# Transposing DMAs issued by ScalarE, reloads in pieces, and one scatter-add per shared slot in a routed decoder layer

## The chip, the cores and the metric

The kernel runs on one core of a Trainium2 chip. The metric is the device time of one execution in microseconds (us), taken as the median of several runs.

## The reference

A decoder layer on x of 8 x 256 tokens of width 256: a gated projection of the normalized rows, a retention over a context, and a feed-forward part in which every token is sent to two of eight experts.

```python
x = x + gate_block(layernorm(x))                     # WB, WBf, gamma = sigmoid(...)
x = x + retention(layernorm(x), ctx, ctx)            # Wq, Wk, Wv, xpos, decay mask
# feed-forward, on u = layernorm(x), added to x with its own skip
xn = rms_norm(u, norm_scale)
scores = einsum('bsd,ed->bse', xn, w_router)
_, ids = top_k(scores, 2); c = softmax(scores) at ids
h = einsum('bsd,ehd->bseh', xn, w_up)                # 8 experts, 2 x 704 columns
val, gate = split(h, 2); h = val * silu(gate)
y = einsum('bseh,edh->bsed', h, w_down)
out = sum over the two experts of a token of y * c, + u
```

## The kernel before

The kernel has three parts. Parts A and B (`step_a`, `step_b`, one step for a batch of 256 tokens) do the gated projection and the retention; B also stores the normalized rows, as fp16 high and low parts, and the softmax values in `xrow_hbm`, and the skip in `out`. The routing chain then sorts the 4096 pairs of token and expert: a chain of small VectorE instructions (`link`, each waits for the one before it), 32 columns of pairs (25 by VectorE, 7 by ScalarE) multiplied on TensorE into the slot table (L1404), from which come `take_idx` (rows to gather) and `add_idx` (rows to add to). A second chain and a product give `slot_expert` and `slot_home`, the expert of each slot and where its weights lie; `s_te` tells that they are ready. TensorE runs filler products (`keep_clock`, L1245) between the groups of this stage.

The expert part has 36 slots of 128 rows in the order `ORDER`. 32 slots belong to one expert. Four are mixed: 64 rows of one expert, 64 of another, with the weights of the second expert copied next to them (`half_up`, `half_dn`). The mixed ones stand at positions 28, 30, 32 and 34. In step r the engines do for slot i = r-1 (`step_e`):

- GpSimd gathers the rows of a slot by an indirect DMA (`take`, L808) into `xs`, two buffers, and adds the result of a slot to `out` by an indirect DMA with addition (L824). Its queue holds in order: wait for `yt` of slot j, wait until the add of slot j-1 has landed, add of j, take of j+4. A take waits for the transposes of the slot two before it.
- SyncE waits for the rows and transposes them by DMA (L485) into `xsT`, two buffers, when the up products of slot i-2 are done. The same queue reloads, step by step, the weights of the experts in the order of their rank (`fetch_up`, 1.4 MB, `fetch_down`), and copies the half weights.
- TensorE: first up product of slot i (L1437), transposes of h of slot i-1 (L1484), the other two up products of slot i, down product of slot i-1 (L1453).
- ScalarE, in this order: y of slot i-2 out of its bank, scaled, into `yt` (L682); silu of the first gate columns (L694); a part of the transposed h (L699); the high part of a reloaded weight (`up_high` L633, `down_high` L639, for r up to 22); silu of the tail (L711); the fp16 high parts of h (L714, L716); in each third step the second half of `down_high`.
- VectorE: the other part of the transposed h (L1183), h = value times silu (L1194), the low parts of h (L1198 to L1201), the scale of the pairs (L1161), the low part of the weights (L917, L923).

A token may have both its experts in the two halves of one mixed slot. An addition DMA that names one row twice would lose one of the two, so a mixed slot is added by two DMAs, one for each half, with the rows of the other half sent to unused rows behind `out` (`half_idx[:, m]`).

## Time and profile before

| | before |
|---|---|
| median of 3 runs | 418.7 us (412.5 to 421.2) |
| the profiled execution | 418.5 us |
| its span | 416.7 us |
| TensorE busy (matmul) | 356.8 us, 86% |
| VectorE, ScalarE, GpSimd busy | 262.8, 235.8, 177.3 us |
| granted clock of TensorE, mean | 0.958 |

The profiler records one execution. The span is the time from its first to its last instruction. The granted clock is the share of its full speed at which TensorE may run. A row of the busy table by stretch has: from and to in us, the length, busy us and count of TensorE's matmuls, of its weight loads, of VectorE, of ScalarE and of GpSimd, then the granted clock, the mean busy share of the 16 DMA engines and the GB/s that they moved. In the other views PE is TensorE, DVE VectorE, ACT ScalarE, POOL GpSimd, SP SyncE; a q behind the name is the engine's queue (register loads, DMA issues). L682 is line 682 of the kernel. An entry in square brackets is the idle time of the engine before the instruction, and what ended it.

### The profile page before, as it was taken

How to read it: one execution, taken by the hardware profiler on the slowest of the kernel's cores; microseconds unless marked ns; L12 is line 12 of the kernel's file. 1: busy time of each engine (PE TensorE's matmuls, PEld its weight loads, DVE VectorE, ACT ScalarE, POOL GpSimd, SP SyncE). 2: the span in 40 equal slices, each digit the busy share in tenths (PEclk: the TensorE clock that was granted, in tenths of full speed). 3: DMA queues.
4: the chain of work that ended last, by engine and by line, in shares of the span. 5: the costliest groups of instructions: out<-in, count | busy, mean ns of one | idle time of the engine just before them, and what ended most of it. 6: DMA issues, size and time to landing. Idle time of an engine off the chain costs nothing.

```text
span 416.7 us, 9007 instructions
## 1 busy us (share of the span) xinstructions
PE 356.8 (86%) x2494; PEld 256.8 (62%) x2494; DVE 262.8 (63%) x714; ACT 235.8 (57%) x432; POOL 177.3 (43%) x183
## 2 busy tenths in 40 slices
PE   5699989999998068797997999899999999988930
PEld 5588878888885053464655566566665666655620
DVE  2799755665567886686676667687775654544410
ACT  3377686677764663575765567577654544433410
POOL 2545544455557302165253434545434334445341
PEclk9899999999999559999999999999999999999995
DMA  7999823444433103968969896444368954776421
GB/s 233 409 424 407 320 101 104 150 153 152 151 102 102 53 5 94 247 178 227 255 170 219 248 226 184 79 78 65 65 177 186 259 71 107 224 207 138 48 28 24
DMA packets 48107, 69.48 MB, mean 167 GB/s; under 512 B 24608, under 2 KB 40864, under 8 KB 46144
## 3 DMA queue, kind: packets, MB, share of 16 engines
q1 hardware_dynamic: 39984, 58.17, 43.1%
q0 software_dynamic: 7536, 10.24, 16.6%
q10 hardware_dynamic: 544, 0.52, 0.4%
q8 instruction: 23, 0.38, 0.4%
q14 instruction: 20, 0.16, 0.1%
HBM read 45.79 MB, written 9.63 MB: 133 GB/s over the span
## 4 chain that ended last, share of the span: by engine, by line
PE 47%; DMA 28%; issue 8%; DVE 7%; POOL 4%; ACT 2%; SPq 1%; DVEq 1%; POOLq 1%; ACTq 0%
PE bank L1437 13%; DMA out<-arena,add_idx 9%; PE bank L1453 6%; DMA out<-arena,half_idx 6%; DMA arena<-xrow_hbm,take_idx 5%; DMA arena<-arena 4%; PE bank L1291 3%; PE bank L1252 3%; PE bank L1254 3%; PE bank L1345 3%; PE bank L1354 3%; PE bank L1484 2%; PE bank L1236 2%; POOL out L824 2%; DMA expert_w<-in_wup 2%
## 5 line engine op out<-in xcount | busy, mean ns | idle before, releaser
L1437 PE MATMUL bank<-expert_w,arena 128*128 x576 | 124.6, 362 | 10.2 <-DMA arena<-arena 9.0
L824 POOL DMA_INDIRECT out<-arena,add_idx x32 | 55.2, 1725 | 107.7 <-ACT arena L682 48.9
L1437 PEld LDWEIGHTS bank<-expert_w,arena 128*128 128x128 f16 x576 | 54.0, 98 | 60.1 <-issue 14.0
L1453 PE MATMUL bank<-expert_w,arena 128*128 x544 | 64.8, 273 | 1.7 <-DVE arena L1183 1.4
L1194 DVE SCALAR_TENSOR_TENSOR arena<-bank,scales,arena 128x512 f32<-128x512 f32 x72 | 41.6, 583 | 34.8 <-ACT arena L711 19.9
L1453 PEld LDWEIGHTS bank<-expert_w,arena 128*128 128x128 f16 x544 | 52.2, 98 | 13.5 <-issue 4.9
L808 POOL DMA_INDIRECT arena<-xrow_hbm,take_idx x36 | 37.8, 1050 | 30.5 <-DVE add_idx L1141 12.6
L694 ACT ACTIVATE arena<-bank,scales 128x512 f32<-128x512 f32 x36 | 24.7, 686 | 43.5 <-PE bank L1437 36.9
L1183 DVE COPY arena<-bank 128x1024 f16<-128x1024 f16 x36 | 24.7, 687 | 18.9 <-PE bank L1484 18.7
L711 ACT ACTIVATE arena<-bank,scales 128x192 f32<-128x192 f32 x36 | 15.1, 420 | 34.0 <-PE bank L1437 25.9
L917 DVE SCALAR_TENSOR_TENSOR expert_w<-expert_w,scales 128x1408 f16<-128x1408 f32 (+2 forms) x18 | 27.1, 1520 | 9.5 <-issue 9.2
L1484 PEld LDWEIGHTS bank<-ident,arena 128*128 128x128 f16 x396 | 24.6, 98 | 12.2 <-ACT arena L716 3.2
L770 POOL TENSOR_TENSOR arena<-arena 128x512 f32<-128x512 f32 x16 | 20.4, 1272 | 23.3 <-DVE arena L1019 18.7
L1484 PE MATMUL bank<-ident,arena 128*128 128x128 f16 x396 | 28.0, 219 | 2.5 <-ACT arena L716 1.7
L633 ACT ACTIVATE expert_w<-expert_w,scales 128x1408 f16<-128x1408 f32 (+1 forms) x16 | 23.4, 1467 | 9.7 <-issue 6.4
L1198 DVE TENSOR_TENSOR arena<-arena 128x512 f16<-128x512 f32 x36 | 24.9, 692 | 4.8 <-ACT arena L714 1.7
L682 ACT ACTIVATE arena<-bank,arena 128x256 f32<-128x256 f32 x36 | 16.9, 469 | 18.1 <-PE bank L1453 15.1
L511 ACT ACTIVATE squares<-expert_w,front 128x1408 bf16<-128x1408 f32 x16 | 23.4, 1460 | 0.0
L714 ACT ACTIVATE arena<-arena 128x512 f16<-128x512 f32 x36 | 22.4, 622 | 1.1 <-DVE arena L1194 1.0
L824 POOL DMA_INDIRECT out<-arena,half_idx x8 | 12.6, 1570 | 21.8 <-DMA out<-arena,half_idx 11.9
L983 DVE TENSOR_TENSOR arena<-bank,cst_b 128x512 f32<-128x512 f32 x16 | 11.0, 690 | 15.3 <-PE bank L1345 11.5
L1252 PE MATMUL bank<-front,arena 128*128 128x258 f32 x64 | 17.5, 398 | 1.0 <-ACT arena L542 1.0
(228 smaller groups left out, 668.0 us busy)
## 6 DMA issues: line engine op xcount, KB each, us to landing
expert_w<-in_wup SPq DMA_DIRECT2D x15, 1408.0 KB, 10.0
expert_w<-in_wdn SPq DMA_DIRECT2D x15, 640.0 KB, 4.4
expert_w<-expert_w SPq DMA_DIRECT2D x4, 704.0 KB, 5.1
expert_w<-in_x SPq DMA_DIRECT2D x8, 256.0 KB, 7.7
arena<-in_ctxT SPq DMA_DIRECT2D x8, 256.0 KB, 3.0
out<-expert_w SPq DMA_DIRECT2D x8, 256.0 KB, 2.5
expert_w<-in_wdn SPq DMA_DIRECT2D x30, 64.0 KB, 4.3
expert_w<-expert_w SPq DMA_DIRECT2D x2, 768.0 KB, 3.6
```

The lines of the kernel that those rows point to most:

```text
L511: nc.scalar.activation(squares[:, 0:2 * H], raw_up(n // 2 + 1, n % 2), ACT.Square, scale=ns_s[:, n % 2:n % 2 + 1], accum_out=sums[:, n:n + ...
L694: nc.scalar.activation(sg[:, 0:HA], bank[0][:, 0:HA], ACT.Silu, scale=gate_scale).then_inc(s_sg, 1)
L808: pool.indirect_dma_start(out=xs_row[:, i % 2], out_offset=None, in_=xrow_hbm, in_offset=bass.IndirectOffsetOnAxis(ap=take_idx[:, ORDER[i] ...
L824: pool.indirect_dma_start(out=out, in_=yt[:, i % 2], in_offset=None, out_offset=bass.IndirectOffsetOnAxis(ap=rows_of, axis=0), compute_op= ...
L917: V.scalar_tensor_tensor(out=up_part(k, c, 1)[:, lo:lo + n], in0=up_source(k, c, e)[:, lo:lo + n], scalar=up_scale[:, ds(e * 2 + c, 1)], i ...
L1183: V.tensor_copy(hT[:, 0:8], hT_bank[0]).then_inc(s_hTa, 1)
L1194: V.scalar_tensor_tensor(out=hh[:, cols], in0=src, scalar=value_scale, in1=sg[:, cols], op0=ALU.mult, op1=ALU.mult).then_inc(s_h, 1)
L1198: V.tensor_tensor(hs_low, hh[:, 0:HA], hs_high[:, 0:HA], ALU.subtract).then_inc(s_hlo, 1)
L1252: T.matmul(dst, uT[:, 2 * slot + c, j * P:(j + 1) * P], wb_s[:, c], start=c == 0, stop=False)
L1437: last = T.matmul(bank[q][:, 0:n], x, split_w[:, ds(home + (c * UPC + at_w), n)], **flags)
L1453: last = T.matmul(y, h, split_w[:, ds(home + dn_at(c, w), D)], **flags)
L1484: last = T.transpose(hT_bank[c // 8][:, c % 8], hs[:, c * P:(c + 1) * P], ident16[:, :])
```

## The change

- `transpose_rows`: the transposing DMAs of slots 1 to 35 leave SyncE's queue and go to ScalarE's. That of slot 1 stands ahead of the first step, that of slot i+2 in the step of slot i, between the tail silu and the fp16 copies, behind a wait for the gathered rows.
- SyncE: one piece per turn. `fetch_up(k, c)` loads one half of the up weights (0.7 MB), so that ranks 1 to 7 are spread over turns 1 to 21 instead of 1 to 14; each half has its own semaphore. The up halves of mixed slots are copied one per turn too.
- Mixed slots: their scaled y goes to `y_mixed`, is multiplied on TensorE by `same_row` (1 where two entries of the slot name the same row of `out`), and is copied from the bank into `yt`. Rows of the upper half that are there twice are sent to an unused row. One addition DMA does the slot. `added(n)` becomes 16 n.
- Routing: the number of the first expert is computed behind the columns, and ScalarE's `up_high` for it, too; the chain of ranks stands behind `add_idx`; the entry constants are computed in step 1 of part B, from a scan in place of a constant; weight scales and routing constants swap their steps; one filler product less.

```diff
         def added(n):
-            return 16 * (n + sum(mixed(i) for i in range(n)))
+            return 16 * n
 
         def dn_at(c, low):
             return 2 * UPC + (c // 3) * DNC + low * DNH + (c % 3) * D
 
-        MARK_LINKS, COL_LINKS, TILE_LINKS, TABLE_LINKS = 13, 34, 35, 48
+        MARK_LINKS, COL_LINKS, TILE_LINKS, TABLE_LINKS = 13, 32, 33, 48
         DVE_COLS = 2 * NT - 7
...
-        HALF_UP_AFTER, HALF_DOWN_AFTER = (23, 25, 30, 32), (24, 26, 31, 33)
+        HALF_UP_AFTER, HALF_DOWN_AFTER = (23, 26, 30, 33), (25, 28, 32, 35)
...
-            def fetch_up(k):
+            def fetch_up(k, c):
                 sp.wait_ge(s_te, 1)
                 sp.wait_ge(s_lo, 4)
                 e = table_entry(slot_expert, UNIFORM + 2 * MIXED + k, NE - 1)
-                sp.dma_start(expert_w[:, (k + 1) * EXP:(k + 1) * EXP + UPC], wup[ds(e, 1)].squeeze(0)).then_inc(s_fup[k], 16)
+                sp.dma_start(raw_up(k + 1, c), wup[ds(e, 1)].squeeze(0)[:, c * 2 * H:(c + 1) * 2 * H]).then_inc(s_fup[k % 2][c], 16)
...
-            def copy_half_up(q):
+                    sp.dma_start(dst[lo:lo + HLAST, tail:DNC], src[0:HLAST, tail:DNC]).then_inc(s_fdn[k % 2], 16)
+
+            def copy_half_up(q, c):
                 if q < 2:
                     sp.wait_ge(s_lo, 2 * NE + 2)
                 else:
                     sp.wait_ge(s_up, 3 * ORDER.index(UNIFORM + q - 2) + 3)
                 home = table_entry(slot_home, UNIFORM + MIXED + q, (NE - 1) * 2 * EXP)
-                for c in range(2):
-                    sp.dma_start(half_up[q % 2][c], split_w[:, ds(home + c * UPC, UPC)]).then_inc(s_hup[q], 16)
+                sp.dma_start(half_up[q % 2][c], split_w[:, ds(home + c * UPC, UPC)]).then_inc(s_hup[q], 16)
 
             def copy_half_down(q):
                 if q < 2:
@@ -479,19 +483,18 @@
                 sp.dma_start(half_dn[q % 2], split_w[:, ds(home + 2 * UPC, 2 * DNC)]).then_inc(s_hdn[q], 16)
 
             for i in range(1, NSLOT):
-                sp.wait_ge(s_xs[i % 2], 16 * (i // 2) + 16)
                 if i >= 2:
                     sp.wait_ge(s_up, 3 * i - 3)
-                sp.dma_start_transpose(xsT[:, i % 2], xs[:, i % 2, 0:4 * P]).then_inc(s_xsT[i % 2], 16)
-                if i <= 2 * (NE - 1):
-                    if i % 2:
-                        fetch_up((i + 1) // 2)
+                if i <= 3 * (NE - 1):
+                    n, part = (i + 2) // 3, (i + 2) % 3
+                    if part < 2:
+                        fetch_up(n, part)
                     else:
-                        fetch_down(i // 2)
+                        fetch_down(n)
                 for q in range(MIXED):
-                    if HALF_UP_AFTER[q] == i:
-                        copy_half_up(q)
-                for q in range(MIXED):
+                    for c in range(2):
+                        if HALF_UP_AFTER[q] + c == i:
+                            copy_half_up(q, c)
                     if HALF_DOWN_AFTER[q] == i:
                         copy_half_down(q)
             sp.wait_ge(s_add, added(NSLOT))
...
-            act.wait_ge(s_first_e, 1)
-            act.wait_ge(s_scl, 9)
-            first = load_expert(first_expert, 0)
-            for c in range(2):
-                up_high(0, c, first)
             act.wait_ge(s_rd, COL_LINKS)
             act.wait_ge(s_xl, NBATCH)
             act.wait_ge(s_rtr, NBATCH)
...
+            act.wait_ge(s_first_e, 1)
+            act.wait_ge(s_scl, 9)
+            first = load_expert(first_expert, 0)
+            for c in range(2):
+                up_high(0, c, first)
             act.wait_ge(s_place, 1)
...
+            def transpose_rows(i):
+                act.wait_ge(s_xs[i % 2], 16 * (i // 2) + 16)
+                act.dma_start_transpose(xsT[:, i % 2], xs[:, i % 2, 0:4 * P]).then_inc(s_xsT[i % 2], 16)
+
+            transpose_rows(1)
 
             def step_e(it, k, r):
                 i = r - 1
@@ -679,8 +688,11 @@
                     act.wait_ge(s_ps, j + 1)
                     if j >= 2:
                         act.wait_ge(s_add, added(j - 1))
-                    nc.scalar.activation(yt[:, j % 2], bank[6 + j % 2][:, 0:D], ACT.Copy,
-                                         scale=pair_scale[:, j:j + 1]).then_inc(s_yt, 1)
+                    if mixed(j):
+                        nc.scalar.activation(y_mixed, bank[6 + j % 2][:, 0:D], ACT.Copy, scale=pair_scale[:, j:j + 1]).then_inc(s_ym, 1)
+                    else:
+                        nc.scalar.activation(yt[:, j % 2], bank[6 + j % 2][:, 0:D], ACT.Copy,
+                                             scale=pair_scale[:, j:j + 1]).then_inc(s_yt, 1)
                 if live(r, 1, NSLOT):
                     act.wait_ge(s_up, 3 * i + 1)
...
+                if live(r, 3, NSLOT) and mixed(j):
+                    act.wait_ge(s_merged, ORDER[j] - UNIFORM + 1)
+                    nc.scalar.activation(yt[:, j % 2], bank[3][:, 0:D], ACT.Copy).then_inc(s_yt, 1)
                 if r in SPLIT_STEPS:
...
+                if live(r, 1, NSLOT - 2):
+                    transpose_rows(i + 2)
                 if live(r, 1, NSLOT):
                     act.wait_ge(s_h, 2 * i + 1)
                     nc.scalar.activation(hs_high[:, 0:HA], hh[:, 0:HA], ACT.Copy).then_inc(s_hhi, 1)
...
             for i in range(NSLOT):
                 pool.wait_ge(s_yt, i + 1)
                 slot = ORDER[i]
-                for m in range(2 if mixed(i) else 1):
-                    if slot == UNIFORM and not m:
-                        pool.wait_ge(s_half, 3)
-                    if i or m:
-                        pool.wait_ge(s_add, added(i) + 16 * m)
-                    rows_of = half_idx[:, m, slot - UNIFORM:slot - UNIFORM + 1] if mixed(i) else add_idx[:, slot:slot + 1]
-                    pool.indirect_dma_start(out=out, in_=yt[:, i % 2], in_offset=None,
-                                            out_offset=bass.IndirectOffsetOnAxis(ap=rows_of, axis=0),
-                                            compute_op=ALU.add).then_inc(s_add, 16)
+                if slot == UNIFORM:
+                    pool.wait_ge(s_half, 8)
+                if i:
+                    pool.wait_ge(s_add, added(i))
+                rows_of = half_idx[:, slot - UNIFORM:slot - UNIFORM + 1] if mixed(i) else add_idx[:, slot:slot + 1]
+                pool.indirect_dma_start(out=out, in_=yt[:, i % 2], in_offset=None,
+                                        out_offset=bass.IndirectOffsetOnAxis(ap=rows_of, axis=0),
+                                        compute_op=ALU.add).then_inc(s_add, 16)
                 if i + 4 < NSLOT:
                     take(i + 4)
...
-                V.tensor_scalar(token, route("padrow"), -float(PADROW + 1), None, ALU.add).then_inc(s_ent, 1)
+                count, number = bank[7][:, 0:P], bank[7][:, P:2 * P]
+                V.tensor_tensor_scan(count, const("ones"), const("ones"), -1.0, ALU.mult, ALU.add).then_inc(s_ent, 1)
                 dve.wait_ge(s_ent, 1)
+                V.tensor_tensor(number, count, ident, ALU.mult).then_inc(s_ent, 1)
+                dve.wait_ge(s_ent, 2)
+                V.tensor_reduce(token, number, AX.X, ALU.add).then_inc(s_ent, 1)
...
                 if r == NBATCH + 2:
-                    weight_scales()
-                    entry_constants()
+                    routing_constants()
...
+                if r == 1:
+                    dve.wait_ge(s_ones, 16)
+                    entry_constants()
                 if r == NBATCH + 1:
-                    routing_constants()
+                    weight_scales()
...
-            link(V.tensor_reduce(entry[:, 0:1], order, AX.X, ALU.max))
-            link(V.tensor_scalar(first_key[:, 0:1], entry[:, 0:1], -1.0, None, ALU.add))
-            V.tensor_scalar(first_expert[:, 0:1], first_key[:, 0:1], NE - 1, NE - 1, ALU.bitwise_and, ALU.bitwise_xor).then_inc(s_first_e, 1)
...
-            dve.wait_ge(s_first_e, 1)
-            first = dve.snap(dve.value_load(first_expert[0:1, 0:1], min_val=0, max_val=NE - 1))
             for n in range(DVE_COLS):
                 V.tensor_scalar(in_col[:, n], column, slot_col[:, n:n + 1], route("tokno")[:, n:n + 1],
                                 ALU.is_equal, ALU.mult).then_inc(s_col32, 1)
 
-            link(V.tensor_reduce(rank, ahead[:, 0], AX.X, ALU.add))
-            link(V.tensor_scalar(rank, rank, -1.0, None, ALU.add))
-            link(V.tensor_scalar(found[:, 0], last_row, entry_slot, None, ALU.is_le))
-            link(V.scalar_tensor_tensor(out=half_key, in0=half_no, scalar=-1.0, in1=odd, op0=ALU.add, op1=ALU.mult))
-            link(V.scalar_tensor_tensor(out=found[:, 1], in0=half_key, scalar=entry_half, in1=rank, op0=ALU.is_equal, op1=ALU.mult))
+            link(V.tensor_reduce(entry[:, 0:1], order, AX.X, ALU.max))
+            link(V.tensor_scalar(first_key[:, 0:1], entry[:, 0:1], -1.0, None, ALU.add))
+            V.tensor_scalar(first_expert[:, 0:1], first_key[:, 0:1], NE - 1, NE - 1, ALU.bitwise_and, ALU.bitwise_xor).then_inc(s_first_e, 1)
 
             table = bank[2][:, 0:NSLOT]
...
+            link(V.tensor_reduce(rank, ahead[:, 0], AX.X, ALU.add))
+            link(V.tensor_scalar(rank, rank, -1.0, None, ALU.add))
+            link(V.tensor_scalar(found[:, 0], last_row, entry_slot, None, ALU.is_le))
+            link(V.scalar_tensor_tensor(out=half_key, in0=half_no, scalar=-1.0, in1=odd, op0=ALU.add, op1=ALU.mult))
+            link(V.scalar_tensor_tensor(out=found[:, 1], in0=half_key, scalar=entry_half, in1=rank, op0=ALU.is_equal, op1=ALU.mult))
             link(V.tensor_reduce(entry[:, 1:3], found, AX.X, ALU.add))
...
                 if r == MIX_STEP + MIXED:
                     V.tensor_copy(half_rows, add_idx[:, UNIFORM:NSLOT]).then_inc(s_half, 1)
                     dve.wait_ge(s_half, 1)
-                    for m, pad in enumerate((pad_upper, pad_lower)):
-                        V.tensor_scalar(half_idx[:, m], half_rows, pad, None, ALU.max).then_inc(s_half, 1)
+                    V.tensor_tensor(row_diag, ident.unsqueeze(1).broadcast_to([P, MIXED, P]),
+                                    half_rows.unsqueeze(2).broadcast_to([P, MIXED, P]), ALU.mult).then_inc(s_half, 1)
+                if r == MIX_STEP + MIXED + 2:
+                    dve.wait_ge(s_same, 1)
+                    V.tensor_tensor(same_row, bank[3][:, 0:MIXED * P].rearrange("p (q n) -> p q n", q=MIXED),
+                                    half_rows.unsqueeze(2).broadcast_to([P, MIXED, P]), ALU.is_equal).then_inc(s_half, 1)
+                    V.tensor_scalar(to_pad, half_rows, -1.0, pad_row, ALU.mult, ALU.add).then_inc(s_half, 1)
+                    dve.wait_ge(s_half, 4)
+                    V.tensor_reduce(twice, same_row, AX.X, ALU.add).then_inc(s_half, 1)
+                    dve.wait_ge(s_half, 5)
+                    V.tensor_scalar(twice, twice, 1.5, upper, ALU.is_ge, ALU.mult).then_inc(s_half, 1)
+                    dve.wait_ge(s_half, 6)
+                    V.tensor_tensor(to_pad, to_pad, twice, ALU.mult).then_inc(s_half, 1)
+                    dve.wait_ge(s_half, 7)
+                    V.tensor_tensor(half_idx[:, :], half_rows, to_pad, ALU.add).then_inc(s_half, 1)
...
-                if n % 4 == 3 and n < DVE_COLS - 1:
+                if n % 4 == 3 and n < DVE_COLS - 4:
...
+                if live(r, 3, NSLOT) and mixed(i - 2):
+                    q = ORDER[i - 2] - UNIFORM
+                    pe.wait_ge(s_ym, q + 1)
+                    if q == 0:
+                        pe.wait_ge(s_half, 3)
+                    else:
+                        pe.wait_ge(s_yt, ORDER.index(UNIFORM + q - 1) + 1)
+                    T.matmul(bank[3][:, 0:D], same_row[:, q], y_mixed, start=True, stop=True).then_inc(s_merged, 1)
+                if r == MIX_STEP + MIXED + 1:
+                    pe.wait_ge(s_half, 2)
+                    T.matmul(bank[3][:, 0:MIXED * P], const("ones"), row_diag.rearrange("p q n -> p (q n)"), start=True, stop=True).then_inc(s_same, 1)
```

## Rows read from the trace of the kernel before

**Rows 1.** Busy table by stretch (columns are explained in the section on the profile).
```profile
136.00:158.00 22.00, 8.24 (x50) 5.75 (x50) 18.89 (x77) 12.15 (x20) 4.20 (x3) 0.54 0.12 28
158.00:262.00 104.00, 91.72 (x670) 58.02 (x670) 72.08 (x129) 65.01 (x111) 41.69 (x30) 1.00 0.81 208
262.00:300.00 38.00, 37.17 (x281) 24.70 (x282) 28.17 (x51) 26.02 (x44) 16.90 (x12) 1.00 0.40 69
```

**Rows 2.** Timeline, one quiet expert step: start us, us, engine, line, operation, [idle].
```profile
268.49 0.92 ACT L639 ACTIVATE expert_w<-expert_w,scales 128x768 f16<-128x768 f32 x1
...
269.32 0.45 ACT L682 ACTIVATE arena<-bank,arena 128x256 f32<-128x256 f32 x1
...
270.05 1.59 POOL L824 DMA_INDIRECT out<-arena,add_idx  x1 [2.95 <-ACT arena L682]
...
271.94 1.04 POOL L808 DMA_INDIRECT arena<-xrow_hbm,take_idx  x1 [0.30 <-issue]
...
273.35 0.42 ACT L711 ACTIVATE arena<-bank,scales 128x192 f32<-128x192 f32 x1 [0.18 <-PE bank L1437]
...
273.67 0.62 ACT L714 ACTIVATE arena<-arena 128x512 f16<-128x512 f32 x1
...
274.26 0.36 ACT L716 ACTIVATE arena<-arena 128x192 f16<-128x192 f32 x1
...
275.11 0.47 ACT L682 ACTIVATE arena<-bank,arena 128x256 f32<-128x256 f32 x1 [0.49 <-PE bank L1453]
...
275.14 0.22 DVE L1201 TENSOR_TENSOR arena<-arena 128x64 f16<-128x64 f32 x1
...
276.20 0.78 PE L1484 MATMUL bank<-ident,arena 128*128 128x128 f16 x11
```

**Rows 3.** SyncE's queue: timeline in that step; its waits, us, times, longest.
```profile
274.82 1.19 SPq L485 DMA_TRANSPOSE arena<-arena  x1
...
SPq L485 <- DMA arena<-xrow_hbm,take_idx: 109.0, 33, 16.4
```

**Rows 4.** Gathers L808, issue to landing; transposing DMAs L485, ns min/median/max.
```profile
DMA to landing us min/median/max: 2.8/3.6/8.6
...
L485 SPq DMA_TRANSPOSE arena<-arena x35: 1189/1227/2149, 161.4 to 386.7; - x35
```

**Rows 5.** The chain of waits: a gather beside a reload; start us, us, what.
```profile
185.34 5.44 DMA arena<-xrow_hbm,take_idx
```

**Rows 6.** A plain DMA in ScalarE's queue at the start of the kernel, timeline.
```profile
1.43 0.63 ACTq L502 DMA_DIRECT2D arena<-in_wproj  x1
```

**Rows 7.** ScalarE's loads of an expert number: duration ns min/median/max.
```profile
L642 ACTq TENSOR_LOAD <-arena x54: 273/279/904, 142.2 to 389.3; - x54
```

**Rows 8.** Timeline of ScalarE: copies of y(0), y(20), y(32) and y(34).
```profile
175.28 0.47 ACT L682 ACTIVATE arena<-bank,arena 128x256 f32<-128x256 f32 x1 [0.55 <-issue]
...
305.53 0.45 ACT L682 ACTIVATE arena<-bank,arena 128x256 f32<-128x256 f32 x1
...
382.52 0.47 ACT L682 ACTIVATE arena<-bank,arena 128x256 f32<-128x256 f32 x1 [0.61 <-PE bank L1451]
...
396.98 0.47 ACT L682 ACTIVATE arena<-bank,arena 128x256 f32<-128x256 f32 x1 [0.61 <-PE bank L1451]
```

**Rows 9.** Timeline of ScalarE: the first copy from a reload.
```profile
172.11 1.47 ACT L633 ACTIVATE expert_w<-expert_w,scales 128x1408 f16<-128x1408 f32 x1 [3.32 <-DMA expert_w<-in_wup]
```

**Rows 10.** The chain of waits in routing: register load by VectorE, TensorE's last filler.
```profile
147.86 0.55 DVEq L1126
...
154.90 0.82 PE bank L1245 x2
```

**Rows 11.** Timeline of ScalarE: the last copy of router scores.
```profile
135.80 0.16 ACT L564 ACTIVATE sc<-bank 128x16 f32<-128x16 f32 x1
```

**Rows 12.** The chain of waits: two products of 128x258 in fp32.
```profile
20.26 0.87 PE bank L1252 x4
```

**Rows 13.** Timeline of GpSimd: the last scatter-add.
```profile
408.55 1.55 POOL L824 DMA_INDIRECT out<-arena,add_idx  x1 [2.97 <-DMA out<-arena,half_idx]
```

40 lines of the change are left out of this document (23 added, 17 removed).

## The prediction

> **What bounds the kernel now.** I read the engine table (in the section on the profile), then the busy table by stretch, then the timeline of one step of the expert part, then the queue of SyncE, then the chain of waits at the end. The engine table shows TensorE busy for 86% of the span. [rows 1] says where it isn't: in routing (136 to 158 us) it does 8.2 us of work in 22 at a granted clock of 0.54, between 158 and 262 us it is busy 91.7 of 104, between 262 and 300 us 37.17 of 38 at full clock. So the quiet expert steps are bound by TensorE, at about 6.0 us a slot, and every other engine has some slack in them. The question for each edit is how much of that slack it uses.
>
> The slack of ScalarE is read in [rows 2], one whole step. At 269.32 ScalarE copies y of a slot out of its bank (L682). That copy releases GpSimd, which issues the scatter-add at 270.05 and, behind it, the gather ("take") of the rows of the slot four later at 271.94. ScalarE goes on: the tail silu L711 at 273.35, the two fp16 copies L714 and L716, and the next y at 275.11. VectorE ends the low parts at 275.14 + 0.22 = 275.36, and TensorE transposes them at 276.20: 0.84 us of slack. [rows 3] shows when the gathered rows have landed: SyncE, which waits for them, starts the transposing DMA at 274.82, and its wait is for the gather in 33 cases, 109 us in all. It has nothing else to do, so that wait costs nothing.
>
> **The one edit that decides: transposing DMAs on ScalarE.** Call the slot in front of ScalarE i. Its step copies y(i-2), which releases take(i+2), since GpSimd issues take(j+4) behind the add of j. The changed step then waits, between L711 and L714, for the rows of take(i+2): the very gather that its own first instruction released. From y to landed rows are 274.82 - 269.32 = 5.50 us (2.62 until the gather starts, 2.88 until it has landed); L711 has ended 4.45 us after y, at 273.77. So in the quietest step ScalarE stands 1.05 us at the wait, and then issues the DMA. What is queued behind it: both copies L714 and L716, for which VectorE's low parts and then TensorE's transposes wait, down_high, and the next y, for which GpSimd's next add and take wait. That closes a ring that no longer has TensorE in it:
>
> y copy to gather start 2.64, gather to landed rows, issue of the transposing DMA, L714 to the next y copy, and again.
>
> Its terms:
> - y to gather start 2.62 to 2.64 [rows 2], as long as the add before has landed, which a step over 8 us leaves time for.
> - Gather to landed: 2.88 in the quiet step [rows 2, 3], median 3.6 of all and up to 8.6 [rows 4], 5.44 in one beside a 1.4 MB reload [rows 5]. SyncE now issues half such a reload per step, when the ups of slot i-2 are done, about 4 to 5 us behind y, when the gather has nearly landed; so I take 3.3 in the steps with reloads, between 2.88 and the median 3.6, and 3.2 later, where half copies of 0.7 MB run. Bounds 2.9 and 5.4.
> - Issue: 1.2 us on SyncE's queue, 1.19 at the least [rows 4]. ScalarE's queue shows no transposing DMA; its nearest row, a plain one, is 0.63 us [rows 6]. I take 1.2, since it is the same instruction; bounds 0.63 and 1.2, and nothing if the queue were free at once.
> - L714 to the next y copy: 0.59 to L716, then the register load of the expert, 0.28 with its index arithmetic and gaps [rows 7], about 1.25 in all; the quiet step shows 1.44 with a wait for TensorE in it [rows 2]. Seven of twenty steps with reloads have one half of down_high there, which starts its 0.92 at 268.49 and lets y follow 0.83 later at 269.32 [rows 2], 1.68 in all, so 1.4 on average.
>
> Step with reloads: 2.64 + 3.3 + 1.2 + 1.4 = 8.54. Later: 2.64 + 3.2 + 1.2 + 1.25 = 8.29. TensorE's own way round is shorter: transposes some 1.85 us behind L714, then 0.61 + 2.27 + 1.87 to the next y, 6.6 in all, so it is covered.
>
> The wait stands in the steps that copy y(0) to y(31), 32 of them. Before, y(0) is at 175.28, y(20) at 305.53, y(32) at 382.52 [rows 8]: 207.2 us, 6.48 each. After: 20 x 8.54 = 170.8 and 12 x 8.29 = 99.5, plus the merge below on two of them, 2 x 1.8 = 3.6: 273.9. **+66.7 us.**
>
> A rule of the Trainium skill bears on this place. [rows 4] has 1.2 us of issue against a landing of some 3 us. The page "DMA: Bandwidth & Descriptors", section "Issuing engines are not separate DMA queues", says that starting DMAs from several engines saves only the time of the sequencer that initiates them, usually small beside the transfer. By that the edit gives SyncE back 1.2 us a slot, which it does not need, and the transfer nothing; with an issue small enough to be called nothing the ring is 7.3 us and the sum about 39 us less. The row says it is not small, and I go by the row.
>
> **Reloads and half copies in pieces.** The reload of rank 1 is now half as large for its first use, and not behind a transposing DMA. Before, ScalarE waited 3.32 us for it at 172.11 [rows 9]. That goes. In its place, in the same two steps, come two transposing issues of 1.2 and the wait for take(3), which itself waits for VectorE's scale of slot 1. Later pieces are issued a step or more ahead of their use (about 8.5 us for 0.7 MB, where 1.4 MB had landed in 7.9), so nothing.
>
> **Routing chain.** Three links of about 0.2 and the register load of the first expert, 147.86 to 148.73, leave the chain to the slot table, and the last group of products loses a filler of 0.82 [rows 10]: about 2.1 us for take_idx. Five links of 0.2 to 0.25 come back ahead of the place table, so the expert table gains 1.0. Weight scales and entry constants leave the last step of the attention part, but the chain there starts with the last router copy of ScalarE, which ends at 135.96 [rows 11], so they give nothing, and the new scan of 128 ones falls in a step where VectorE idles. All this brings slot 0 about 1.5 us forward. With the 3.32 above against the two issues (2.4) and the later take(3), I put y(0) where it was: 0, with -3 and +3 as bounds.
>
> **The merge.** Four scatter-adds go. For each mixed slot come a second copy of 0.47 on ScalarE, a product of 128x256 in fp32 of 0.43 (0.87 for two of 258 columns [rows 12]) on TensorE, and once a product of 512 columns and eight VectorE instructions, under 4 us, all inside the idle time that the ring leaves. What isn't hidden is the time from y to the scatter-add: TensorE takes the product behind its transposes, so yt is ready 1.8 us later. In the steps of y(28) and y(30) this sits in the ring (the 3.6 above).
>
> At the end it pays. The two steps from y(32) to y(34) took 396.98 - 382.52 = 14.46 because takes were held up behind adds; without, 6.0 + 0.43 + 6.2 = 12.7: **-1.8**. From y(34) to the end were 416.7 - 396.98 = 19.7: two adds of half rows, then the last at 408.55 [rows 13], each some 4.5, and 4.4 behind its landing. Now add(34) starts 2.5 behind y(34), lands 4.1 later, the last starts 0.3 later, lands in 3.8, and 4.4 to the end: 15.0. **-4.7.**
>
> **Sum** against the profiled span: 416.7 + 66.7 + 0 - 1.8 - 4.7 = 476.9. The profiled execution took 418.5 with that span, and the median of the runs is 418.7, so 2 us are added: **479 us**.
>
> **Rivals.**
> - A, cheap issue: ScalarE's queue is held 0.6 us or less, and the gathers land in 2.9. Ring 2.64 + 2.9 + 0.63 + 1.3 = 7.47, with the 3.6 of the merge 242.6 for 32 steps, +35.4: 448. For it: the row of a plain DMA. Against: the same instruction never took under 1.19 on SyncE.
> - B, gathers stay as slow as in the reload stage: 5.4 in 20 steps and 3.6 in 12: (10.64 x 20) + (8.69 x 12) + 3.6 = 320.7, +113.5: 526. For it: the bytes are the same. Against: the step is longer, the piece smaller and issued behind the gather.
> - C, the other side: the rows have landed when ScalarE comes by, and the issue costs it next to nothing. Then TensorE stays the bound at 6.0, the reload steps lose their 0.5 us of waits, and the end gives 6.5: 416.7 - 10 - 6.5 + 2 = 402. It decides from the point at which y to landed rows is under 4.45; the quiet step has 5.50, and [rows 3] has SyncE wait for the gather in 33 of 35 steps. It needs a path from y to gather that is over 1 us shorter, and nothing in the change shortens it.
> - D, no change that can be told: issue nothing and the quiet landing throughout, ring 2.64 + 2.88 + 1.3 = 6.82, with the merge 221.8 for 32 steps, +14.6, against -6.5: 427.
> - The clock: idle gaps of 2 us per step might lower it. [rows 1] has full clock between 158 and 262 us, with TensorE idle 12% of the time. Not priced.
>
> **Chances.** The forecast with its own range 460 to 505: 0.78. A 0.08, B (or between) 0.07, D 0.04, C 0.03. The range 450 to 515 leaves out the far ends of A, B, and C and D. Over 2% faster 0.03, within 2% 0.03, over 2% slower 0.94; 2% is about what a measurement of this kernel can tell from no change, its three runs lying between 412.5 and 421.2.
>
> **What would show it.** Right: ScalarE idle ahead of L714 in nearly each step, put down to the gather; y copies 8 to 9 us apart between y(0) and y(32); TensorE busy under 80% there; a transposing issue near 1.2 on ScalarE's queue; only 36 scatter-adds, and under 16 us from y(34) to the end. Wrong: if y copies stay near 6.1 to 6.5 apart, the ring does not bind. If the issue is near 0.6, A. If the rows land over 5 us behind the gather, B. take_idx should come near 154.0 instead of 156.1, whatever the rest does.

## The result and the profile after

| | before | after |
|---|---|---|
| median of the runs | 419.17 us (4 runs, 412.5 to 421.15) | 479.96 us (4 runs, 478.57 to 481.48) |
| span of the profiled execution | 416.7 us | 479.5 us |
| mean granted clock | 0.958 | 0.945 |
| TensorE busy in the span | 86% | 78% |

The ratio of after to before is 1.154, 95% interval 1.145 to 1.162. The prediction was 479 us, with 450 to 515 as its range. Some executions of a kernel are a few per cent longer at a lower clock; the ratios here and below leave them out, the medians don't.

The engine table and the costliest groups of the profile after (the part on busy time, and the part on groups: line, engine, operation, xcount | busy us, mean ns | idle time before it and what ended most of it):

```profile
PE 375.4 (78%) x2502; PEld 258.1 (54%) x2502; DVE 264.6 (55%) x720; ACT 236.7 (49%) x436; POOL 173.2 (36%) x179
...
PE 27%; DMA 24%; issue 19%; ACTq 7%; DVE 7%; ACT 7%; POOL 7%; POOLq 0%; DVEq 0%; SPq 0%
DMA arena<-xrow_hbm,take_idx 15%; DMA out<-arena,add_idx 7%; ACTq L677 7%; POOL out L840 5%; PE bank L1472 3%; PE bank L1326 3%; PE bank L1380 3%; PE bank L1287 3%; PE bank L1289 3%; PE bank L1389 3%; ACT arena L731 2%; PE bank L1271 2%; ACT arena L694 2%; DMA arena<-in_w 1%; PE bank L1338 1%
...
L840 POOL DMA_INDIRECT out<-arena,add_idx x32 | 51.0, 1595 | 166.1 <-ACT arena L694 143.3
...
L1519 PE MATMUL bank<-ident,arena 128*128 128x128 f16 x396 | 29.7, 227 | 61.0 <-ACT arena L733 55.6
L731 ACT ACTIVATE arena<-arena 128x512 f16<-128x512 f32 x36 | 22.6, 629 | 97.2 <-issue 93.3
```

TensorE has lost its place in the chain: it holds 27% of it (47% before), and DMAs, issue and ScalarE's queue hold half. The last three lines are one story told by three engines. ScalarE stands 93.3 us ahead of its first fp16 copy (L731; L714 of before), where the new wait and issue are. TensorE stands 55.6 us ahead of its transposes for those copies, and GpSimd 143.3 us ahead of its scatter-adds for y (L694; L682 of before). ScalarE's wait is put down to "issue" there. What it really was is read from the chain of waits of the kernel after (start us, us, what), which holds the same three links again and again:

```profile
219.60 1.58 POOL out L840
221.49 2.84 DMA arena<-xrow_hbm,take_idx
224.34 1.22 ACTq L677
227.53 1.54 issue
229.08 3.44 DMA arena<-xrow_hbm,take_idx
232.53 1.21 ACTq L677
```

Gather, transposing issue on ScalarE, then the next gather. One link between them is ScalarE's own, in its timeline of the same step:

```profile
222.29 0.42 ACT L726 ACTIVATE arena<-bank,scales 128x192 f32<-128x192 f32 x1
224.34 1.22 ACTq L677 DMA_TRANSPOSE arena<-arena  x1
225.62 0.63 ACT L731 ACTIVATE arena<-arena 128x512 f16<-128x512 f32 x1 [2.90 <-issue]
226.15 0.35 ACT L733 ACTIVATE arena<-arena 128x192 f16<-128x192 f32 x1
226.41 0.46 ACT L694 ACTIVATE arena<-bank,arena 128x256 f32<-128x256 f32 x1
```

The tail silu L726 has ended at 222.71; the gather started at 221.49 and its rows are there at 224.33; the transposing DMA is issued at 224.34; L731 follows at its end. The 2.90 us of idle time are 1.63 us of waiting for the gather and 1.22 us of issue. VectorE and TensorE are behind it (timelines of the same step):

```profile
226.28 0.69 DVE L1220 TENSOR_TENSOR arena<-arena 128x512 f16<-128x512 f32 x1 [3.03 <-ACT arena L731]
...
227.41 0.77 PE L1519 MATMUL bank<-ident,arena 128*128 128x128 f16 x11 [1.66 <-ACT arena L733]
```

The ring of the prediction is closed. The y copies that answer to [rows 8], of y(0), y(20), y(32) and y(34):

```profile
176.79 0.46 ACT L694 ACTIVATE arena<-bank,arena 128x256 f32<-128x256 f32 x1
...
346.38 0.45 ACT L694 ACTIVATE arena<-bank,arena 128x256 f32<-128x256 f32 x1
...
452.15 0.46 ACT L692 ACTIVATE squares<-bank,arena 128x256 f32<-128x256 f32 x1
...
464.97 0.47 ACT L692 ACTIVATE squares<-bank,arena 128x256 f32<-128x256 f32 x1 [0.61 <-PE bank L1486]
```

From these, in the terms of the prediction, the whole difference of the two spans (479.5 - 416.7 = 62.8 us) is: y(0) 1.5 later (176.79 against 175.28), y(0) to y(32) in 275.4 instead of 207.2, +68.1, and y(32) to the end in 27.35 instead of 34.18, -6.8. A span is that of one execution. In the runs that the ratios use, the spans of the kernel before lie between 412.6 and 418.8 us, so a difference of two spans of a few us is within what executions scatter, unless a stretch of the trace shows where it arises.

### The profile page after: what moved, and what is told of

Same layout as the page of the kernel before. It is cut to its first block, busy times and chain, and to the rows that moved or that the text cites. A ratio compares the mean times of both kernels' runs of the same rounds, so it can differ in the third digit from the quotient of the medians.

```text
span 479.5 us, 9079 instructions
## 1 busy us (share of the span) xinstructions
PE 375.4 (78%) x2502; PEld 258.1 (54%) x2502; DVE 264.6 (55%) x720; ACT 236.7 (49%) x436; POOL 173.2 (36%) x179
## 4 chain that ended last, share of the span: by engine, by line
PE 27%; DMA 24%; issue 19%; ACTq 7%; DVE 7%; ACT 7%; POOL 7%; POOLq 0%; DVEq 0%; SPq 0%
DMA arena<-xrow_hbm,take_idx 15%; DMA out<-arena,add_idx 7%; ACTq L677 7%; POOL out L840 5%; PE bank L1472 3%; PE bank L1326 3%; PE bank L1380 3%; PE bank L1287 3%; PE bank L1289 3%; PE bank L1389 3%; ACT arena L731 2%; PE bank L1271 2%; ACT arena L694 2%; DMA arena<-in_w 1%; PE bank L1338 1%
## 5 line engine op out<-in xcount | busy, mean ns | idle before, releaser
L1472 PE MATMUL bank<-expert_w,arena 128*128 x576 | 134.6, 382 | 1.2 <-ACT arena L672 0.9
L840 POOL DMA_INDIRECT out<-arena,add_idx x32 | 51.0, 1595 | 166.1 <-ACT arena L694 143.3
L1472 PEld LDWEIGHTS bank<-expert_w,arena 128*128 128x128 f16 x576 | 57.3, 103 | 56.6 <-issue 19.9
L1519 PE MATMUL bank<-ident,arena 128*128 128x128 f16 x396 | 29.7, 227 | 61.0 <-ACT arena L733 55.6
L731 ACT ACTIVATE arena<-arena 128x512 f16<-128x512 f32 x36 | 22.6, 629 | 97.2 <-issue 93.3
L1488 PE MATMUL bank<-expert_w,arena 128*128 x544 | 65.5, 274 | 6.0 <-DVE arena L1205 3.2
L1488 PEld LDWEIGHTS bank<-expert_w,arena 128*128 128x128 f16 x544 | 50.6, 98 | 23.6 <-issue 16.9
L825 POOL DMA_INDIRECT arena<-xrow_hbm,take_idx x36 | 44.1, 1225 | 33.6 <-DVE arena L1181 13.4
L1216 DVE SCALAR_TENSOR_TENSOR arena<-bank,scales,arena 128x512 f32<-128x512 f32 x72 | 40.8, 581 | 26.2 <-PE bank L1472 11.6
L726 ACT ACTIVATE arena<-bank,scales 128x192 f32<-128x192 f32 x36 | 15.2, 421 | 43.6 <-PE bank L1472 35.5
L933 DVE SCALAR_TENSOR_TENSOR expert_w<-expert_w,scales 128x1408 f16<-128x1408 f32 (+2 forms) x18 | 27.1, 1521 | 10.3 <-issue 9.1
L711 ACT ACTIVATE arena<-bank 128x384 f16<-128x384 f16 x36 | 17.7, 491 | 19.2 <-PE bank L1519 14.2
L636 ACT ACTIVATE expert_w<-expert_w,scales 128x1408 f16<-128x1408 f32 (+1 forms) x16 | 23.4, 1467 | 5.5 <-issue 5.5
L514 ACT ACTIVATE squares<-expert_w,front 128x1408 bf16<-128x1408 f32 x16 | 23.4, 1460 | 0.0
L1271 PE MATMUL bank<-cst,arena 128*128 128x128 f32 x96 | 15.3, 283 | 3.7 <-ACT arena L535 2.3
L939 DVE SCALAR_TENSOR_TENSOR expert_w<-expert_w,scales 128x768 f16<-128x768 f32 (+1 forms) x16 | 15.6, 1015 | 4.3 <-issue 4.3
```

Source lines behind the costliest of these rows:

```text
L731: nc.scalar.activation(hs_high[:, 0:HA], hh[:, 0:HA], ACT.Copy).then_inc(s_hhi, 1)
L825: pool.indirect_dma_start(out=xs_row[:, i % 2], out_offset=None, in_=xrow_hbm, in_offset=bass.IndirectOffsetOnAxis(ap=take_idx[:, ORDER[i] ...
L840: pool.indirect_dma_start(out=out, in_=yt[:, i % 2], in_offset=None, out_offset=bass.IndirectOffsetOnAxis(ap=rows_of, axis=0), compute_op= ...
L933: V.scalar_tensor_tensor(out=up_part(k, c, 1)[:, lo:lo + n], in0=up_source(k, c, e)[:, lo:lo + n], scalar=up_scale[:, ds(e * 2 + c, 1)], i ...
L1216: V.scalar_tensor_tensor(out=hh[:, cols], in0=src, scalar=value_scale, in1=sg[:, cols], op0=ALU.mult, op1=ALU.mult).then_inc(s_h, 1)
L1271: last = T.transpose(dst[:, c * SEQ + j * P:c * SEQ + (j + 1) * P], src(j, c), ident)
```

## The experiments

All times below are medians of the runs with the median of the kernel before on the same chip beside it, or one time where only one profiled execution was taken. "Step" is the distance between two y copies, as a mean from y(0) to y(20) and from y(20) to y(32).

### 1. The change without its one move (e1_transposes_on_sync)

```diff
-            def transpose_rows(i): ...            # ScalarE, and its two calls
             for i in range(1, NSLOT):             # SyncE
+                sp.wait_ge(s_xs[i % 2], 16 * (i // 2) + 16)
                 if i >= 2:
                     sp.wait_ge(s_up, 3 * i - 3)
+                sp.dma_start_transpose(xsT[:, i % 2], xs[:, i % 2, 0:4 * P]).then_inc(s_xsT[i % 2], 16)
```

> The changed kernel with its transposing DMAs back on SyncE, all else of the change kept. Ring theory (ScalarE waits in its own step for the gather that its own y copy released): the ring is gone, steps fall from 8.5 to 8.8 us to 6.0 to 6.4, and what stays of the change is worth -2.5 in routing, -6.5 at the end and some 3 in the reload stage: 405 to 410 us. Rival 1 (pieces of reloads or fewer bytes per turn starve TensorE): still above 450 us. Rival 2 (the merge costs TensorE and ScalarE in every step): steps stay over 7 us near slots 28 to 35 and the end does not get shorter.

Measured: 412.31 us against 417.73, ratio 0.989 (0.985 to 0.992), span 410.8. Steps 6.51 and 6.53 where the whole change has 8.48 and 8.81; y(0) at 170.40. So one move carries the loss (479.5 - 410.8 = 68.7 us of span), and all the rest together is a small gain. The time is 2 us over the expected range. Against the three terms expected (-2.5, -3 and -6.5), y(0) came 4.9 earlier, y(0) to y(32) took 1.4 longer, and the end was 2.4 shorter, because y(32) to y(34) took 17.15 instead of 12.7. TensorE stood there for half a copy of weights, which SyncE's later turns had issued late, and its clock then fell to the lower level. A timeline line, and then windows (stretch, its length, busy us of PE, PEld, DVE, ACT and POOL with instruction counts, granted clock, DMA share, GB/s) of this kernel:

```profile
381.42 0.63 PE L1464 MATMUL bank<-expert_w,arena 128*64 x1 [2.46 <-DMA arena<-expert_w]
...
377.00:381.40 4.40, 1.96 (x34) 1.69 (x34) 1.75 (x6) 1.74 (x4) 0.13 (x1) 0.97 0.75 224
381.40:385.00 3.60, 3.58 (x24) 1.82 (x24) 0.00 (x0) 0.69 (x1) 0.00 (x0) 0.56 0.62 228
```

### 2. The move alone, on the kernel before (e2_only_transposes_moved)

```diff
-                sp.wait_ge(s_xs[i % 2], 16 * (i // 2) + 16)          # SyncE
-                sp.dma_start_transpose(xsT[:, i % 2], ...)
+                if live(r, 1, NSLOT - 2):                            # ScalarE, ahead of the fp16 copies
+                    transpose_rows(i + 2)
```

> The kernel before with only the transposing DMAs moved to ScalarE. Ring theory: steps of 8.5 us or more from y(0) to y(32), and without the gains of the merge and of routing 485 to 495 us; with reloads of 1.4 MB in 14 turns the gathers of the first half land later than 3.4 us. Rival (the loss needs the rest of the change too): near 420 us.

Measured: 500.13 us against 417.73, span 498.2, 5 us over the expected range. Steps 8.90 and 9.28. The move alone costs 81.5 us of span; with the rest of the change around it, 68.7. In the first twenty steps the issue started 3.79 us behind its gather instead of 3.36. A reload of up weights goes out here as one block of 1.4 MB and not in halves, and one gather (181.36 us), between such a block issued at 176.38 and down weights issued at 182.93, had 10.8 us to the issue behind it and a step of 16.1. That one gather is nearly the whole difference: the nineteen steps behind it take 8.52 us in the mean, against 8.49 in the kernel after. So in the first twenty steps the pieces are worth at most the 7.9 us of that one step, and the ring itself is as long without them.

### 3. The gather ahead of the scatter-add (e3_gather_ahead_of_add)

A rival to "the issue and the wait on ScalarE cost this" was that the length of the ring does, wherever it is shortened. Here GpSimd, once y is copied, issues the gather first and the add behind it.

```diff
                 pool.wait_ge(s_yt, i + 1)
+                if i + 4 < NSLOT:
+                    take(i + 4)
                 slot = ORDER[i]
                 ... scatter-add of slot i ...
-                if i + 4 < NSLOT:
-                    take(i + 4)
```

> The changed kernel with GpSimd's gather of slot j+4 ahead of the scatter-add of slot j, still behind the wait for y of slot j. Ring theory with its terms: y to gather start falls from 2.67 to 0.8, the wait for the rows is over about when the tail silu is, and the step falls by some 1.9 to 6.6 us: 418 to 424 us. Rival (ScalarE is simply 1.2 us per slot too busy, 36 issues = 43 us, whatever the gather does): no change, 480 us.

Measured: 471.71 us, span 469.9, steps 8.21 and 8.39. A miss by 50 us. In the first twenty steps, from y to the gather were 1.49 us in the mean instead of the expected 0.8, and from gather to issue 4.07, in the kernel after 3.36. The waits of this kernel (180 to 390 us: who waited for what, us in all, times, longest) and the timelines of GpSimd and VectorE name the reason:

```profile
POOL arena L825 <- DVE arena L1181: 87.7, 19, 6.9
...
300.64 2.41 POOL L825 DMA_INDIRECT arena<-xrow_hbm,take_idx  x1 [4.06 <-DVE arena L1181]
...
298.66 0.69 DVE L1220 TENSOR_TENSOR arena<-arena 128x512 f16<-128x512 f32 x1 [2.34 <-ACT arena L731]
...
299.70 0.16 DVE L1181 TENSOR_TENSOR arena<-arena,scales 128x1 f32 x1
300.49 1.69 DVE L933 SCALAR_TENSOR_TENSOR expert_w<-expert_w,scales 128x1408 f16<-128x1408 f32 x1 [0.64 <-issue]
```

The gather overwrites a buffer of rows that VectorE's pair scale (L1181) reads last, and VectorE issues that scale behind the three low parts, which wait for ScalarE's L731, which stands behind the transposing issue. So there is a second ring of nearly the same length, by VectorE instead of by y, and the add in front of the gather had been hiding it. And the issue of the gather itself, 1.05 us in the step shown of after, takes 2.41 here: VectorE's L933 ends at 302.18, and the issue ends 0.87 us behind that, at 303.05. This is no single case. L933 and L939 (L917 and L923 of before, and their like in the other kernels; they make the low parts of the weights) run at the start of 152 gathers in the fourteen traces, and 145 of these issues end 0.82 to 0.94 us behind the end of that instruction. The other seven took 0.97 to 0.99 us. The 352 gathers issued beside none of them have a median of 0.99 us, and ten took over 1.15.

### 4. The transposing DMA behind the fp16 copies (e4_transpose_behind_copies)

```diff
-                if live(r, 1, NSLOT - 2):
-                    transpose_rows(i + 2)
                 ... the two fp16 copies L731, L733 ...
+                if live(r, 1, NSLOT - 2):
+                    transpose_rows(i + 2)
```

This tells "ScalarE's copies come late" (then this version recovers most) from "y, and the next gather with it, comes late" (then it recovers little).

> The changed kernel with ScalarE's wait and transposing DMA behind the two fp16 copies of h instead of ahead of them. Ring theory: the wait still stands between one y copy and the next, only the 0.5 to 0.8 us of the copies leave the ring: steps of 7.9 to 8.1, 460 to 468 us. Rival (what costs is that the fp16 copies, and so TensorE's transposes, come late): they are on time again, steps of 6.1 to 6.6, 410 to 425 us.

Measured: 488.66 us, span 486.8, clock 0.912, steps 8.95 and 8.88: nothing is recovered. That refutes the first reading, as I had expected, but the size was a miss by 20 us. The first thirteen steps fall in two kinds: 7.4 to 7.95 us where the gather landed in 2.8 to 3.2 us, and 10 to 11.6 where it took 5 to 6. Behind them the steps are 7.5 to 10.6, with landings of 2.8 to 5.8. One of the second kind (GpSimd, SyncE's queue and ScalarE in time):

```profile
275.18 1.61 POOL L840 DMA_INDIRECT out<-arena,add_idx  x1 [4.99 <-ACT arena L694]
...
276.91 0.35 SPq L465 DMA_DIRECT2D expert_w<-in_wdn  x1
277.09 0.99 POOL L825 DMA_INDIRECT arena<-xrow_hbm,take_idx  x1 [0.30 <-issue]
...
277.80 1.16 SPq L467 DMA_DIRECT2D expert_w<-in_wdn  x2
278.01 0.36 ACT L731 ACTIVATE arena<-arena 128x192 f16<-128x192 f32 x1
...
283.32 1.22 ACTq L677 DMA_TRANSPOSE arena<-arena  x1
285.69 0.47 ACT L694 ACTIVATE arena<-bank,arena 128x256 f32<-128x256 f32 x1 [7.32 <-issue]
```

The copies are done at 278.4, and then ScalarE stands until the rows have landed, 6.2 us behind the gather's start, with y behind it. SyncE's reload goes out in the same microsecond as the gather here; in the step shown of the kernel after it goes out at 222.90, 1.4 us behind the gather's start, which then had landed after 2.84. The lateness of y alone keeps the ring closed. Weights beside the gather aren't all of it: the one at 401.88 landed in 4.3 us with none issued within 4 us of it.

### 5. The same with thin reloads (e11_behind_copies_thin_reloads)

If the reload beside the gather makes the long steps, they must go with its bytes. The reloads of ranks 1 to 7 carry only their first 64 columns here; the rest of those weights is left out, so that the output isn't the reference's.

```diff
-  ...dma_start(out=<weights of the rank>, in_=in_wup[...])
+  ...dma_start(out=<weights of the rank>[:, 0:64], in_=in_wup[...][:, 0:64])     # and in_wdn
```

> The version with ScalarE's wait and transposing DMA behind the fp16 copies, with the reloads of ranks 1 to 7 cut to their first 64 columns each (the rest of the weights is left out, so its output is not the reference's). It gave steps of 7.4 to 7.9 us where the gather landed in 2.8, and 10 to 11.6 where it landed in 5 to 6. If the reload piece issued beside the gather made it late: gathers in 2.8 to 3.3, steps of 7.5 to 7.9 up to y(20), 460 to 466 us. If something else made it late (the lower clock, the adds): steps stay at 8.9 and the time at 488.

Measured: 471.8 us, span 470.0, 6 us over the expected range, steps 8.23 and 8.84. The first thirteen steps are 7.6 to 8.1 us (one 8.8) with gathers that land in 2.8 to 3.3, as expected of the bytes; the landing time of all gathers has a median of 3.0 instead of 3.8. But some later gathers still have 3.9 to 6.05 us to the transposing issue behind them. The one with 6.05 has a copy of half weights issued 0.4 us ahead of it, and these copies are not thinned here. Three more, at 276.93, 293.89 and 310.55, have only thin pieces beside them and 3.9 to 4.3 us, and one at 383.64 has no weights issued within 4 us and 4.7. So without the reload's bytes the long steps among the first thirteen are gone. As the thin pieces mostly went out 1.5 to 2.2 us ahead of the gather there, and not in its microsecond, the bytes and the moment weren't taken apart; and what makes those four later gathers slow stays open.

### 6. The gather freed from y and from the scale, with the transposes on ScalarE (e5_gather_free_scale_early)

The ring needs y ahead of the gather only because GpSimd issues in order, and the scale late only because VectorE does. Both orders are changed here, and the transposing DMAs stay on ScalarE.

```diff
             for i in range(NSLOT):                       # GpSimd
+                if i + 4 < NSLOT:
+                    take(i + 4)
                 pool.wait_ge(s_yt, i + 1)
                 ... scatter-add of slot i ...
-                if i + 4 < NSLOT:
-                    take(i + 4)
             def step_e(it, k, r):                        # VectorE
                 i = r - 1
+                if live(r, 0, NSLOT) and r > 0:
+                    expert[r] = scale_pairs(r)           # moved up from the end of the step
```

> The changed kernel, transposing DMAs on ScalarE as in the change, with both ways round opened: GpSimd issues the gather of slot j+4 before it waits for y of slot j, and VectorE takes the scale of a slot (for which that gather also waits) at the start of its step instead of behind the low parts. What is left of the move is its issue on ScalarE's queue, 1.2 us per slot between the tail silu and the fp16 copies, against 0.84 us of slack. Ring theory: the wait ahead of the fp16 copies goes, steps of 6.3 to 6.6 us, 410 to 422 us. Rival (ScalarE is too busy with the issue itself, not waiting): steps stay above 7.5 us, 450 us or more.

Measured: 427.03 us against 417.86, ratio 1.026 (1.019 to 1.033), span 425.4, steps 6.73 and 7.22; 5 us over the expected range. The gather now starts 2.7 us ahead of the y copy it used to follow. This gives back 54 of the 68.7 us with the transposing DMAs still where the change put them, each still 1.2 us on ScalarE. So most of the loss is the closed ring. What is left of the move costs the rest, and experiment 7 measures it. It is not the issue alone: from 180 to 390 us ScalarE still stands seven times, 17.0 us in all with the issues of 1.2 in it, at the place of the wait, and GpSimd's gather waits 16 times, 28.0 us in all, until an earlier transposing DMA has read its buffer:

```profile
POOL arena L825 <- DMA arena<-arena: 28.0, 16, 3.5
...
ACT arena L731 <- issue: 17.0, 7, 3.8
```

### 7. The same with the transposes back on SyncE (e6_sync_gather_free)

Experiments 1 and 6 together.

> The same, with the transposing DMAs on SyncE: no issue on ScalarE either. The difference to the kernel with them on ScalarE is the price of the issue alone, by the ring theory 0.2 to 0.5 us a slot, 7 to 16 us in all. Against the version with transposes on SyncE and gathers as they were (412 us, steps of 6.5): if late gathers and transposes caused its stalls, steps of 6.2 to 6.3 and 402 to 406 us; if late reload pieces caused them, no change.

Measured: **398.35 us** against 417.86, ratio 0.958 (0.952 to 0.964), span 395.5. This beats both kernels, and the expected 402 to 406. Its window from 170 to 370 us, below that of experiment 6 from 180 to 390 (columns as in experiment 1):

```profile
170.00:370.00 200.00, 199.22 (x1611) 131.69 (x1610) 137.46 (x293) 122.89 (x224) 98.32 (x64) 1.00 0.79 182
```
```profile
180.00:390.00 210.00, 194.11 (x1503) 122.02 (x1501) 129.87 (x276) 118.03 (x212) 82.46 (x61) 1.00 0.74 161
```

TensorE is busy 199.2 of 200 us: the expert part is bound by its matmuls and by nothing else, at 6.04 us a step up to y(20) and 6.38 behind. With the transposes on ScalarE it is busy 92% of the time. The two kernels differ in nothing but the queue of the transposing DMAs, and by 29.9 us of span: y(0) 6.3 us earlier, 0.68 us a step up to y(20), 0.83 behind (24 in 32 steps). I had expected 7 to 16. The 0.84 us of slack of [rows 2] are not enough to swallow an issue of 1.21: it stands ahead of the fp16 copies, for which VectorE and TensorE wait. This is the price of the edit once the ring is open, with the seven late gathers in it.

By the page "DMA: Bandwidth & Descriptors" of the Trainium skill, section "Issuing engines are not separate DMA queues", initiating DMAs on several engines saves only the time that the sequencer takes to initiate them, "which is usually small relative to the DMA itself". In these two runs the issuing engine is all that differs, and that time isn't small: 1.21 us of it on ScalarE, with the waits that go with it, cost 0.7 to 0.8 us a step.

### 8. The add's place with an early scale (e12_ahead_of_add_scale_early)

Experiment 3 had two faults at once; this is experiment 3 with the scale at the start of VectorE's step, so that the ring by VectorE is open and the one by y, shortened, is left.

> The changed kernel with the gather ahead of the add (still behind y), as in the run that gave 472 us, and the scale of a slot at the start of VectorE's step. If that run was held by a second way round (fp16 copies of ScalarE, low parts and scale of VectorE, gather, transposing DMA), opening it gives y to gather start 0.8, steps of 6.6 to 7.3 and 425 to 440 us. If not, 470 us again.

Measured: 446.16 us, span 444.4, steps 7.51 and 7.47. Between experiment 3 (469.9) and experiment 6 (425.4): the early scale is worth 25.5 us of span, freeing the gather from y another 19. The expected range is missed by 6. From y to the gather are 0.75 us as expected, but from the gather to the issue behind it 4.33 in the mean instead of 3.4. In its timeline:

```profile
252.41 1.04 POOL L825 DMA_INDIRECT arena<-xrow_hbm,take_idx  x1 [2.93 <-ACT arena L694]
254.43 1.59 POOL L842 DMA_INDIRECT out<-arena,add_idx  x1 [0.97 <-DMA out<-arena,add_idx]
259.12 1.22 ACTq L677 DMA_TRANSPOSE arena<-arena  x1
```

A scatter-add is issued 2.0 us behind this gather, and the issue that waits for the rows starts 6.7 us after the gather. In the kernel after the add had gone ahead of the gather. What the ring gained at one link it gave back in part at the next. The add's place doesn't explain it by itself: an add stands 1.3 to 2.6 us behind each of these gathers, and half of the 32 have only 3.1 to 3.8 us to the issue. The six that have 5.6 to 6.7 all have a piece of weights issued 2.2 to 3.3 us ahead of them (here 2.2), but so have others with 3.3 to 3.6 us. So the cause stays open.

### 9. The turns of the pieces (e7_sync_turns_as_before, e8_sync_turns_gather_free)

The turns of SyncE as before (both halves of a reload in one turn of two, half copies two to a turn), with the transposes on SyncE; first on the change as it is, and then with the gathers free. The halves stay two DMAs with a semaphore each, so these runs test the turns and not the halving.

```diff
-                if i <= 3 * (NE - 1):
-                    n, part = (i + 2) // 3, (i + 2) % 3     # one piece a turn, 21 turns
+                if i <= 2 * (NE - 1):                       # two halves in one turn of two
```

> The changed kernel with the transposing DMAs on SyncE and the reloads and half copies in the turns of the kernel before (both halves of a reload in one turn, 14 turns; half copies at 23 to 33): what stays is the merge and the routing chain. If the pieces in 21 turns come too late for steps of 6 us (ScalarE waited 10.5 us for them, TensorE 2.5 us for the last half copy), this is 4 to 8 us faster than the version with pieces: 404 to 408 us. If the pieces help, it is slower than 412 us.

> Both: transposes on SyncE, turns of the kernel before, gathers free of y and the scale early. If late gathers and late pieces are separate causes the gains add: 396 to 403 us. If one hides the other it equals the better of the two.

Measured: 415.79 us against 417.86 for the first (ratio 0.989, 0.983 to 0.994; ten runs of 408 to 422), which with the pieces spread over the turns was 412.31 against 417.73, the same ratio. The second: 402.22 against 417.86, ratio 0.965 (0.958 to 0.972), span 400.0, steps 6.25 and 6.42. So I was wrong to take the late half copy of experiment 1 as a net loss of the spread turns: they cost nothing that can be told, and once TensorE is the bound they are worth 4.5 us of span (400.0 - 395.5; medians 402.22 and 398.35, of four runs each). The second is within what I had expected, the first is not. In the 170 to 370 us of experiment 7 and of this kernel, GpSimd waits for earlier scatter-adds to land (us in all, times, longest):

```profile
POOL out L837 <- DMA out<-arena,add_idx: 17.1, 6, 3.7
```
```profile
POOL out L837 <- DMA out<-arena,add_idx: 45.2, 14, 6.2
```

### 10. The merge alone (e9_merge_alone)

Transposes, turns and routing chain as before; the merge of the double rows is left of the change, with the entry constants in step 1 of part B, and the reload halves as two DMAs in one turn.

> Transposes on SyncE, turns and routing chain as in the kernel before, the merge kept (with the entry constants in step 1 of part B, which it needs): the merge alone. By the traces: the stretch from y(32) to the end was 34.2 us before and 27.5 in the versions with the merge, so 412 us, 1.2 to 1.8% under the kernel before. Rival (its products and copies cost in the steps of slots 28 to 35): no gain, 418 us.

Measured: 416.11 us against 419.02 (ten runs of 408 to 424), ratio 0.981 (0.975 to 0.986), span 410.6. From y(32) to the end are 27.6 us, before 34.2: -6.6, where the prediction had -1.8 and -4.7. There is one scatter-add a mixed slot instead of two. The rest of the span is not the merge's: y(0) is 2.8 us earlier, with ScalarE's wait of 3.32 us for the first reload gone, and y(0) to y(32) takes 3.3 us more.

### 11. The kernel before with free gathers (e10_before_gather_free)

The edit of experiment 6 on the kernel before.

> The kernel before with two edits only: the gather of slot j+4 ahead of the wait for y of slot j, and the scale of a slot at the start of VectorE's step. If the stalls of the reload stage (steps of 6.5 instead of 6.04) come from gathers that are tied to y, 408 to 411 us. The end stays as it was, with eight adds of half rows. Rival (they come from the reloads): 418 us.

Measured: 410.86 us against 419.02, ratio 0.981 (0.977 to 0.985), span 408.5, steps 6.07 and 6.46. From there to experiment 7 the span falls by 13.0 us: 3.4 up to y(0), 1.3 in the steps, and 8.2 behind y(32), of which the merge has most (experiment 10). Of the 3.4, 1.9 stand at the end of the attention part already, which is scatter (see y(0) below). So the change holds three useful edits (merge, routing order, and, once the gathers are free, the spread turns), which the move of the transposes hid.

## Why the prediction was right, and where it wasn't

**The ring, right, term by term.** y to the gather 2.64, measured 2.67 as a mean of twenty steps. Gather to landed 3.3, measured 3.36; it lay between 2.8 and 4.9, and the 5.4 of [rows 5] never came. Issue 1.2, measured 1.21 on ScalarE's queue, so that rival A (0.63) is out: a transposing DMA holds ScalarE as long as it holds SyncE. From the start of the issue to L731 1.34 and from there to the next y 1.11, together 2.45 where the prediction had 2.6. Step 8.54, measured 8.48.

**The 3.3 was right for another reason, which is luck.** The prediction put the 0.4 us above the quiet 2.88 down to the reload beside the gather. In the kernel after, the gathers of the first twenty steps are of two kinds. Seven were issued in 1.04 to 1.06 us and landed in 2.9 in the mean, though a piece of a reload was issued 1.4 to 1.6 us behind the start of each. Thirteen took 1.4 to 1.9 us to issue, each until 0.86 to 0.87 us behind the end of VectorE's L933, and landed in 3.6. One of the thirteen has no reload near it, and landed in 3.38 all the same:

```profile
330.55 1.69 DVE L933 SCALAR_TENSOR_TENSOR expert_w<-expert_w,scales 128x1408 f16<-128x1408 f32 x1 [0.63 <-issue]
331.51 1.58 POOL L825 DMA_INDIRECT arena<-xrow_hbm,take_idx  x1 [0.30 <-issue]
```

So what lengthened this link is mostly the issue on GpSimd beside VectorE's work on a weight, and hardly the bytes of the reload. That the pieces go out in the right place, 1.4 to 2.2 us behind the gather's start in most steps, still matters: issued in the same microsecond they made landings of 5 to 6 us (experiment 4).

**The later steps, too short by 0.2.** Predicted 8.29 and 0.3 a step for the merge, measured 8.81. Most of it is the gather, which took 3.40 there, not 3.2. The rest is "In the steps of y(28) and y(30) this sits in the ring", right in place and mis-sized: from y to the gather were 4.86 and 4.87 us, 2.2 more than in the others, not 1.8, which is under 0.1 a step.

**y(0), 1.5 later instead of 0, and closer than it deserves.** Three stretches give it. The attention part ends 2.2 us earlier in this execution (GpSimd's last instruction of 1.01 us there starts at 129.08 instead of 131.28), and that is scatter: over all traces it starts between 128.99 and 131.44 with the change's code, and between 129.37 and 131.40 with the code of before. From there to the first gather are 23.4 us in each of the ten traces with the new routing chain and 25.9 in each of the four with the old one, so the chain gives 2.5 (predicted 2.1 for take_idx, which was written at 151.39 instead of 156.08). From the first gather to y(0) are 24.28 us instead of 18.09, 6.2 longer, where the prediction had the 3.32 of the vanished wait against 2.4 of issues and a late take(3), about nothing. With the transposes back on SyncE that stretch has 16.15 us (experiment 1). So the vanished wait gave some 1.9 and not 3.3, and the transposing DMAs on ScalarE cost 8.1 us ahead of y(0), or 6.7 between experiments 6 and 7 (24.32 against 17.63): that term was the one mis-sized. Without the scatter y(0) would have been 3.7 later, beyond the bound of 3. One link of it in the chain after is the gather of slot 2, beside the two reload pieces issued at 160.70:

```profile
160.46 4.88 DMA arena<-xrow_hbm,take_idx
165.36 1.21 ACTq L677
```

**The clock, not priced, and it fell.** The prediction left it out on the strength of [rows 1]. Before, the granted clock was at 1.00 from 158 to 404 us. After, it fell to the lower level in six stretches between 157 and 448 us. Windows of the kernel after show two of them with what came ahead, and one without a fall:

```profile
209.00:212.00 3.00, 1.04 (x13) 0.84 (x14) 1.54 (x5) 2.16 (x5) 1.18 (x1) 1.00 0.48 143
212.00:215.40 3.40, 3.40 (x11) 1.45 (x10) 2.68 (x3) 1.20 (x2) 1.88 (x2) 0.50 0.46 71
...
440.00:444.00 4.00, 0.84 (x4) 0.20 (x2) 0.35 (x1) 1.01 (x3) 0.00 (x0) 1.00 0.66 230
444.00:447.40 3.40, 2.62 (x15) 1.75 (x16) 1.53 (x5) 1.39 (x3) 2.50 (x2) 0.51 0.21 19
...
292.50:295.50 3.00, 0.70 (x5) 0.17 (x3) 1.16 (x4) 1.83 (x4) 0.00 (x0) 1.00 0.99 237
```

TensorE had done 1.04 us of work in 3.0 ahead of the first and 0.84 in 4.0 ahead of the second. Such a gap doesn't decide it alone: the last window has 0.70 us of work in 3.0, and the clock stayed at its upper level there and until 389 us. What decides it stays open. In the ring this cost little, since TensorE waits there anyway: the step from y(4), copied at 210.07, took 8.80, against 8.88 for the one from y(1), which also has a half of down_high and ran at full clock. Ahead of y(0), where two of the six lie, it may have cost more. From the first gather to y(0) were 16.15 us in experiment 1, without a fall there, and 17.4 to 17.7 in experiments 7 and 9 with one of 3.4 us; they differ in the turns or in the order of the gathers too, so some 1.4 us a fall is an estimate from these runs, and it was not tried apart.

**SyncE's wait, called free, wasn't.** "It has nothing else to do, so that wait costs nothing" holds for the quiet step that it was read from, and not for the kernel. In the profile before, TensorE's first up products wait 9.0 us in all for the transposes that stand behind it:

```profile
L1437 PE MATMUL bank<-expert_w,arena 128*128 x576 | 124.6, 362 | 10.2 <-DMA arena<-arena 9.0
```

Freeing the gathers on the kernel before, with the scale early, took 8.2 us off its span (experiment 11). The forecast didn't suffer, since the ring covers this wait.

**The end, right.** y(32) to y(34) 12.82 (predicted 12.7), y(34) to the end 14.5 (15.0).

**The rivals.** B, C and D needed a landing of 5.4, a path under 4.45 or an issue of nothing, and the chain shows 6.0 from y to rows and 1.21 of issue. C's 402 us stand for rows that have landed when ScalarE comes by and an issue that costs next to nothing; experiment 6 makes nearly the first and has 427, so the second fails too. Without the ring, the kernel would still have paid 0.7 to 0.8 us a step (experiment 7).

The sum came within 3 us of the span: 476.9 against 479.5, which is 1.5 missing at y(0) and 1.4 in the ring (68.1 against 66.7), less the 0.3 that the end gained beyond the forecast (-6.8 against -6.5). So small a difference is partly luck: the first twenty steps were 1.2 us too long and the twelve behind them 2.7 too short, and 2.2 us of scatter hid most of the miss at y(0).

## What to carry to other kernels

Before moving a wait to another engine, follow it back: if what it waits for is released by an earlier instruction of the same engine, the path from release to wait is a floor under the step, and it is added up link by link from the trace before (here 8.54 against 8.48 measured, each link within 0.15). The remedy is as often the order of the releasing engine as the place of the wait: issuing the gather ahead of a wait it doesn't need gave back 54 of 69 us. And look for the second dependence behind the first; shortening only the one by y (experiment 3) gave 10 us instead of 54. Two executions of one kernel can also differ by more than the terms that one wants to read: here the attention part alone ended up to 2.4 us apart with the same code, so compare stretches that start at a common event.

## What the runs showed that I had not expected

- An issue of 1.21 us on an engine with 0.84 us of slack a step cost 0.68 to 0.83 us a step, and 6.3 us in the first slots (experiments 6 and 7).
- The issue of an indirect gather holds GpSimd for 0.94 to 1.1 us alone. Where VectorE is in the middle of making a weight's low part (L933, L939), the issue ends 0.82 to 0.94 us behind the end of that instruction, in 145 of 152 cases, and so takes up to 2.4 us (experiment 3). The traces show this coupling in time; no run removed only that instruction, and why it is so isn't shown.
- A gather of 128 rows lands in 2.8 us at the least. It landed in 6.2 with a reload issued in the same microsecond (experiment 4) and in 10.8 between 1.4 MB issued 5.0 us ahead and 0.6 MB issued 1.6 us behind (experiment 2); landings of 3.9 to 4.7 with no such bytes near them stay unexplained (experiment 5).
- TensorE's clock falls in the middle of a kernel that keeps it busy 78% of its span: between 162 and 448 us five times in the kernel after, each time for 3.4 to 7 us, and never between 162 and 389 us in experiment 7, where TensorE has no idle time. In the windows shown, 2 to 3 us without work lie ahead of a fall, and in one as much without a fall behind it.
